# First attention of an eight-sublayer kernel: two score passes in one loop over head pairs, float32r parts in 64-row halves, values for four heads at a time

## Chip, cores and metric

One Trainium2 chip, one of its cores. The metric is the time of one execution on the device, in microseconds (us). The kernel before took 2060.26 us (median of 3 runs, 2055.55 to 2063.94).

## The reference, cut to what matters

The program applies eight sublayers to x (8 batches of 256 rows of 256). The change touches the first one alone:

```python
xn = layernorm(x)                                   # (8, 256, 256)
qh = (xn  @ Wq.T + bq) in 16 heads of 16
kh = (ctx @ Wk.T + bk) in 16 heads of 16
vh = (ctx @ Wv.T + bv) in 16 heads of 16
scores = einsum('bhqd,bhkd->bhqk', qh, kh) / sqrt(16)
scores = where(mask[:, None] == 0, -1e10, scores)
x = x + softmax(scores) @ vh (heads side by side) @ Wo.T + bo
```

Then come a routed feed-forward layer with 8 experts, a causal attention with 16 heads of 64, a second expert layer, a product without softmax, a linear layer, an attention with one head of 256, and a quantised feed-forward layer with a convolution.

## The kernel before

Each sublayer is a stage of its own with a block of engine programs and a barrier behind it. The first attention is `attention0`; a layer norm stands before it and one behind it. It works on one batch of 256 rows at a time. TensorE is written `pe`, VectorE `dve`, ScalarE `act`, GpSimd `pool` and SyncE `sp`.

**Parts.** Queries and keys are projected in float32 (`project`, L313) and split into three bfloat16 parts (high L447, rest L499, middle L452, low L505). DMAs stack copies of the parts on top of each other, six bands of 16 rows per head, so that one product over 96 rows gives a score to nearly float32 accuracy (`to_stack`, L228: 12 DMAs for queries on SP's queue, 12 for keys on GpSimd's).

**Two score passes.** The softmax's maxima are needed before its exponentials. Pass one (`scores`, L338) makes scores with queries on the partitions; a product of an identity with a bfloat16 mask (L340) adds a huge negative number where the mask is zero; DVE reduces each pair of heads (a unit, 8 units in a batch) to its row maxima (L523). The maxima are turned (L347), split into three bfloat16 rows (L457 to L532) and moved by DMA under the stacked queries (`shift_rows`, L263). Pass two (`weigh`, L363 with the mask at L365) makes the scores again, transposed, with the maximum already subtracted by those rows; ACT takes exponentials out of PSUM into `pT` (L467), one unit at a time.

**Values.** For each unit, products of `V` with `pT` (L376) give 32 columns of output per head. Two heads of a unit go to two different column groups of TensorE. One column of V is one, so that it gives the softmax's sum. DVE takes the four banks' worth out in two copies (L541), DMAs turn the sums (L269), DVE inverts them (L515), DMAs put them back as rows (L273), a product with `sel` spreads them (L384), DVE multiplies (L550), and the output projection (L391) is added to x (L557).

**Order.** In a batch TensorE runs: project the next batch, `weigh` for this batch, `scores` for the next, spread the sums, turn the next batch's maxima, output. PSUM banks 0 to 3 are two pairs for a unit each, and both passes alternate between them. Loops over pairs of batches (`Fori`) hold the first six batches; stacked parts, masks and V have two buffers.

Of the kernel before, what the change touches and what calls it, by code (L numbers as in the profile page):

```python
# [21 lines left out]
P = 128  # L22
B, S, D = 8, 256, 256
DK = D // P
# [141 lines left out]
def attention0(nc, top, x, xt, io, consts):  # L166

    G, NG, W = 4, H // 4, 32
    U = H // 2
    PARTS = ((0, 0, 0, 1, 1, 2), (0, 1, 2, 0, 1, 0))
    R = len(PARTS[0]) * D0  # L180
    LAND = 16 * 2 * len(PARTS[0])
    HB = P // D0
    with top.stage() as ctx:
        def sb(name, shape, dt=F32):
# [9 lines left out]
        neg, negT = sb("neg", [P, 2, TB, S], BF16), sb("negT", [P, 2, TB, S], BF16)  # L194
        part = sb("part", [P, 3, 2, DK, S], BF16)
        rest = sb("rest", [P, 2, DK, S])
        qs, ks = sb("qs", [P, 2, H, S], BF16), sb("ks", [P, 2, H, S], BF16)
        V = sb("V", [P, 2, TB, H, W])
        top_s = sb("top_s", [P, TB, H])
        mpart, mrest = sb("mpart", [H, 3, S], BF16), sb("mrest", [H, S])  # L200
        pT = sb("pT", [P, 2, 2, TB, S])
# [4 lines left out]
        O = ps[:, 4:6, :].rearrange("p a (c n) -> p (a c) n", c=2)  # L206

        (weights, ctx_in0, ctx_in1, mask_in, ones_set, q_proj, k_proj, v_proj, hi_done, rest_done, mid_done, lo_done,
         stacked, v_out, neg_ready, s_ready, max_done, mt_ready, mhi_done, mrest_done, mmid_done, mlo_done,
         mrow_landed, st_ready, exp_done, pv_done, o_out, sums_landed, recip_landed, l_ready, recip_done, norm_done,  # L210
         wo_ready, resid_done) = (
             top.semaphore("a0_" + n) for n in (
                 "weights", "ctx_in0", "ctx_in1", "mask_in", "ones_set", "q_proj", "k_proj", "v_proj", "hi_done",
                 "rest_done", "mid_done", "lo_done", "stacked", "v_out", "neg_ready", "s_ready", "max_done",
                 "mt_ready", "mhi_done", "mrest_done", "mmid_done", "mlo_done", "mrow_landed", "st_ready",
                 "exp_done", "pv_done", "o_out", "sums_landed", "recip_landed", "l_ready", "recip_done", "norm_done",
                 "wo_ready", "resid_done"))
        gate, gate_set = sb("gate", [1, 4]), top.semaphore("a0_gate_set")
# [4 lines left out]
        def to_stack(engine, w, n, s):  # L223

            for t, which in enumerate(PARTS[w]):
                if which == n:
                    for k in range(DK):
                        engine.dma_start((qs, ks)[w][t * D0:(t + 1) * D0, s, k * HB:(k + 1) * HB, :],  # L228
                                         part[:, n, w, k, :]).then_inc((stacked, k_stacked)[w], 16)

        def every_batch(engine, body):

            with engine.Fori(0, B // 2 - 1) as pair:
                body(pair * 2, 0, pair, False)
                body(pair * 2 + 1, 1, pair, False)
            body(B - 2, 0, B // 2 - 1, False)
            body(B - 1, 1, B // 2 - 1, True)

        @block.sync
        def _(sp):  # L240
            sp.sem_inc(stacked, 16)
            sp.sem_inc(mrow_landed, 16)

            def load(b, s):
                sp.wait_ge(v_proj, b + 1)
                sp.dma_start(ctxT[:, s, :, :], io["ctxT"][bass.ds(b, 1)].rearrange("b (k p) s -> p (b k) s", p=P)
                             ).then_inc(ctx_in[s], 16)
                sp.wait_ge(neg_ready, b + 1)
                sp.dma_start(mask[:, :, :], io["mask"][bass.ds(b, 1)].rearrange("b (t p) s -> p (b t) s", p=P)
                             ).then_inc(mask_in, 16)  # L250
                sp.dma_start(maskT[:, :, :], io["maskT"][bass.ds(b, 1)].rearrange("b (t p) s -> p (b t) s", p=P)
                             ).then_inc(mask_in, 16)

            def stack(b, s):

                for n, ready in enumerate((hi_done, mid_done, lo_done)):
                    sp.wait_ge(ready, b * 2 + 1)
                    to_stack(sp, 0, n, s)

            def shift_rows(b, s):  # L260
                sp.wait_ge(mlo_done, b + 1)
                for n in range(3):
                    sp.dma_start(qs[R + n:R + n + 1, s, :, :], mpart[:, n, :]).then_inc(mrow_landed, 16)  # L263

            def turn_sums(b):

                sp.wait_ge(o_out, b * 2 + 2)
                for g in range(G):
                    sp.dma_start(sums[g * W:(g + 1) * W, :], oraw[g * W + D0:g * W + D0 + 1, :, :]  # L269
                                 ).then_inc(sums_landed, 16)  # L270
                sp.wait_ge(recip_done, b + 1)
# [4 lines left out]
            def feed(b, s):  # L276

                sp.wait_ge(pv_done, b * U + 2)
                stack(b + 1, 1 - s)
                turn_sums(b)  # L280
                shift_rows(b + 1, 1 - s)

            for dst, name in ((wq, "a0_wq"), (wk, "a0_wk"), (wv, "a0_wv"), (wo, "a0_wo")):
                sp.dma_start(dst[:, :, :], io[name].rearrange("k p n -> p k n")).then_inc(weights, 16)
            sp.dma_start(bqk[:, :, :], io["a0_bqk"]).then_inc(weights, 16)
            for dst, name in ((bv, "a0_bv"), (sel, "a0_sel")):
                sp.dma_start(dst[:, :], io[name]).then_inc(weights, 16)
            load(0, 0)
            load(1, 1)
            stack(0, 0)  # L290
            shift_rows(0, 0)
            with sp.Fori(0, B // 2 - 1) as pair:
                for s in range(2):
                    load(pair * 2 + (2 + s), s)
                    feed(pair * 2 + s, s)
            feed(B - 2, 0)
            turn_sums(B - 1)

        @block.tensor
        def _(pe):  # L300
            pe.sem_inc(v_proj, 2)
            pe.sem_inc(pv_done, 2)
            pe.sem_inc(l_ready, 1)
            pe.sem_inc(wo_ready, 1)
            pe.wait_ge(weights, 16 * 7)

            def project(b, s, half, left=1):
                pe.wait_ge(ctx_in[s], half * 16 + 16)
                pe.wait_ge(norm_done, left)
                for n, (w, src, done) in enumerate(((wq, xt, q_proj), (wk, ctxT, k_proj))):  # L310
                    for c in range(DK):
                        for k in range(DK):
                            mm = pe.matmul(ps[:, 6 + n, c * S:(c + 1) * S], w[:, k, c * P:(c + 1) * P],  # L313
                                           xt[:, k, bass.ds(b * S, S)] if src is xt else ctxT[:, s, k, :],
                                           start=(k == 0), stop=(k == DK - 1))
                    mm.then_inc(done, 1)
                pe.wait_ge(rest_done, b * 2 + 1)
                for t in range(TB):
                    for k in range(DK):
                        mm = pe.matmul(ps[:, 6, t * S:(t + 1) * S], ctxT[:, s, k, t * P:(t + 1) * P], wv[:, k, :],  # L320
# [3 lines left out]
            def scores(b, s, before):  # L324

                pe.wait_ge(stacked, (b + 1) * LAND + 16)
                pe.wait_ge(k_stacked, (b + 1) * LAND)
                pe.wait_ge(neg_ready, b + 2)
                pe.wait_ge(ones_set, 5)
                for u in range(U):  # L330
                    if u >= 2:
                        pe.wait_ge(max_done, b * U + (u - 1))
                    elif before is not None:
                        pe.wait_ge(exp_done, before * U + (U - 1 + u))
                    for j in range(2):
                        h, bank = 2 * u + j, ps[:, 2 * (u % 2) + j, :]
                        for t in range(TB):
                            pe.matmul(bank[:, t * S:(t + 1) * S], qs[0:R, s, h, t * P:(t + 1) * P], ks[0:R, s, h, :],  # L338
                                      start=True, stop=False)
                            mm = pe.matmul(bank[:, t * S:(t + 1) * S], consts["identb"][:, :], neg[:, s, t, :],  # L340
                                           start=False, stop=True)
                    mm.then_inc(s_ready, 1)

            def turn_maxima(b):
                pe.wait_ge(max_done, b * U + U)
                for t in range(TB):
                    mm = pe.transpose(ps[0:H, 4, t * P:(t + 1) * P], top_s[:, t, :], consts["ident"][:, :])  # L347
# [1905 lines left out]
```

## Time and profile before

| | |
|---|---|
| median of 3 runs | 2060.26 us |
| the profiled execution's own time | 2058.89 us |
| its span in the profile | 2057.0 us |
| mean granted TensorE clock | 0.881 |
| PE, PEld busy (share of the span) | 1567.8 us (76%), 1342.9 us (65%) |
| DVE, ACT, POOL busy | 874.1 us (42%), 551.1 us (27%), 337.0 us (16%) |
| first attention, first DMA to last DVE instruction | 28.56 to 368.28 us |

PE is TensorE's matmuls, PEld its weight loads. Busy shares are over the whole span; the first attention is about a sixth of it. PEclk is the granted TensorE clock as a share of 2.4 GHz. A float32 matmul of the program appears as two MATMUL records. The "x8" of a row counts records.

### The profile page before, as it was taken

To read this page: it belongs to the slowest core of one execution; us is meant where nothing else is said; L and a number is where in the kernel's file an instruction comes from. 1 tells how busy PE (TensorE), PEld (TensorE's weight loads), DVE (VectorE), ACT (ScalarE), POOL (GpSimd) and SP (SyncE) were. 2 spreads that over 40 slices of the span, in tenths; PEclk is the share of its full clock that TensorE was granted. 3 is DMA by queue.
4 is the path that set the end of the run, shared out by engine and by line. 5 is a ranking of instruction groups with operands and counts; after the bars stand their busy time and mean duration, and the time that the engine had idled before them with its cause. 6 is when DMAs were issued, how large, how long until landed. Compare 5 with 4: busy or idle time off the path is not lost. (4 is left out here: it accounts for less than half of the span.)

```text
span 2057.0 us, 32700 instructions
## 1 busy us (share of the span) xinstructions
PE 1567.8 (76%) x11346; PEld 1342.9 (65%) x11346; DVE 874.1 (42%) x1913; ACT 551.1 (27%) x1311; POOL 337.0 (16%) x401
## 2 busy tenths in 40 slices
PE   2799997539991699999994099999999256691775
PEld 2465564429991588888884099999999245581664
DVE  5453542402224566666665011111111235548896
ACT  1233232102211455444441011111111011221553
POOL 1112120020002333232321400000000511004122
PEclk8899999569996799999995599999999668795787
DMA  4344241158132200000003454224470210101000
GB/s 123 62 74 67 48 67 14 59 197 275 41 112 77 70 6 7 7 7 2 2 1 113 147 196 148 99 70 147 148 270 18 76 43 20 34 26 41 6 16 21
DMA packets 118240, 152.13 MB, mean 74 GB/s; under 512 B 15360, under 2 KB 101376, under 8 KB 118016
## 3 DMA queue, kind: packets, MB, share of 16 engines
q1 hardware_dynamic: 101536, 123.86, 19.6%
q0 software_dynamic: 7680, 18.89, 4.2%
q10 hardware_dynamic: 8928, 8.13, 1.1%
q8 instruction: 56, 0.92, 0.2%
q14 instruction: 40, 0.33, 0.1%
HBM read 113.16 MB, written 24.64 MB: 67 GB/s over the span
## 5 line engine op out<-in xcount | busy, mean ns | idle before, releaser
L1271 PE MATMUL f_ph<-f_xgT,f_w 128*128 128x128 f32 x3232 | 375.2, 277 | 19.0 <-DMA f_w<-in_f_w 17.8
L1271 PEld LDWEIGHTS f_ph<-f_xgT,f_w 128*128 128x128 f32 x3232 | 373.8, 194 | 24.2 <-issue 21.4
L1281 PE MATMUL f_py<-f_w,f_hT 128*128 128x256 f32 x992 | 224.5, 379 | 0.0
L1281 PEld LDWEIGHTS f_py<-f_w,f_hT 128*128 128x128 f32 x992 | 183.7, 190 | 22.6 <-issue 0.2
L1342 DVE TENSOR_TENSOR f_hT<-f_ph,f_gate_o 128x512 f32<-128x512 f32 x78 | 53.9, 691 | 309.7 <-ACT f_gate_o L1305 309.7
L1376 POOL DMA_INDIRECT c_yt<-sorted_y,dest x48 | 45.6, 949 | 653.2 <-issue 653.2
L799 ACT ACTIVATE a_work<-a_ps,a_bias 128x128 f32<-128x128 f32 (+1 forms) x256 | 104.1, 419 | 145.4 <-DVE a_bias L879 128.2
L937 POOL TENSOR_TENSOR a_work<-a_work,a_recip 128x256 f32<-128x256 f32 (+1 forms) x128 | 103.1, 826 | 233.1 <-DVE a_recip L894 233.1
L145 PE MATMUL n_tp<-ident,n_xn 128*128 128x128 f32 x160 | 32.2, 371 | 135.2 <-DVE n_xn L125 134.5
L1305 ACT ACTIVATE f_gate_o<-f_ph 128x512 f32<-128x512 f32 x78 | 46.6, 597 | 295.2 <-PE f_ph L1271 295.1
L145 PEld LDWEIGHTS n_tp<-ident,n_xn 128*128 128x128 f32 x160 | 24.7, 189 | 143.1 <-DVE n_xn L125 136.1
L1260 PE MATMUL f_px<-ident,f_xg 128*128 128x128 f32 x124 | 24.3, 278 | 90.6 <-DMA f_xg<-sorted_x 90.6
L899 DVE TENSOR_TENSOR a_qk<-a_ps,a_qk 128x512 fp32r<-128x512 f32 x64 | 44.2, 691 | 103.9 <-ACT a_qk L818 103.9
L523 DVE TENSOR_REDUCE a_top_s<-a_ps 128x4 f32<-128x1024 f32 x64 | 75.7, 1214 | 16.7 <-PE a_ps L340 15.9
L467 ACT ACTIVATE a_pT<-a_ps 128x1024 f32<-128x1024 f32 x64 | 64.6, 1023 | 57.6 <-PE a_ps L365 57.6
L338 PE MATMUL a_ps<-a_ks,a_qs 96*128 96x256 bf16 x256 | 62.1, 280 | 22.9 <-DMA a_qs<-a_part 13.5
L1260 PEld LDWEIGHTS f_px<-ident,f_xg 128*128 128x128 f32 x124 | 15.7, 144 | 91.1 <-DMA f_xg<-sorted_x 91.1
L1349 DVE TENSOR_SCALAR f_hT<-f_ph,f_b 128x128 f32<-128x128 f32 x92 | 25.9, 344 | 114.6 <-PE f_ph L1271 114.6
L1173 POOL DMA_INDIRECT sorted_x<-xn,dest x48 | 46.4, 966 | 168.8 <-DVE dest L1149 154.8
L376 PE MATMUL a_ps<-a_pT,a_V 128*32 128x256 f32 x512 | 67.7, 385 | 2.8 <-ACT a_pT L467 1.8
L661 PE MATMUL a_ps<-a_src,a_wq_high 128*128 128x256 f32 x256 | 53.4, 291 | 17.4 <-DVE a_wk_low L843 14.6
L876 DVE TENSOR_REDUCE a_top_s<-a_ps 128x2 f32<-128x256 f32 (+1 forms) x128 | 64.4, 544 | 5.3 <-PE a_ps L724 5.3
(307 smaller groups left out, 3104.8 us busy)
## 6 DMA issues: line engine op xcount, KB each, us to landing
f_w<-in_f_w SPq DMA_DIRECT2D x72, 1024.0 KB, 7.1
f_xg<-sorted_x SPq DMA_DIRECT2D x62, 128.0 KB, 2.1
sorted_y<-f_yg ACTq DMA_DIRECT2D x62, 128.0 KB, 1.7
a_qs<-a_part SPq DMA_DIRECT2D x96, 64.0 KB, 5.2
a_ks<-a_part POOLq DMA_DIRECT2D x96, 64.0 KB, 5.5
sorted_x<-zeros SPq DMA_DIRECT2D x1, 4992.0 KB, 16.4
a_ctxT<-in_ctxT SPq DMA_DIRECT2D x16, 256.0 KB, 2.8
sorted_x<-zeros SPq DMA_DIRECT2D x1, 2944.0 KB, 10.2
```

The source lines that it names most:

```text
L145: mm = pe.transpose(tp[:, b % SLOTS, k, t * P:(t + 1) * P], xn[:, row if router else row % (SLOTS * TB), k * P:(k + 1) * P], ident[:, :])
L338: pe.matmul(bank[:, t * S:(t + 1) * S], qs[0:R, s, h, t * P:(t + 1) * P], ks[0:R, s, h, :], start=True, stop=False)
L376: mm = pe.matmul(O[W * (g0 + j):W * (g0 + j + 1), n, :], V[:, s, t, 4 * n + g0 + j, :], pT[:, m % 2, j, t, :], start=(t == 0), stop=(t == ...
L467: act.activation(pT[:, u % 2, :, :, :].rearrange("p j t n -> p j (t n)"), ps[:, 2 * (u % 2):2 * (u % 2) + 2, :], ACT.Exp, scale=float(D0) ...
L523: dve.tensor_reduce(top_s[:, :, 2 * u:2 * u + 2].rearrange("p t j -> p j t"), ps[:, 2 * (u % 2):2 * (u % 2) + 2, :].rearrange("p j (t k) - ...
L661: mm = pe.matmul(out, left[a][c], right[b][c], start=start and i == 0, stop=stop and i == len(todo) - 1)
L799: act.activation(prob[:, s, i, t * P:(P if t == 0 else TRI)], ps[:, SB + 2 * s + i, t * S:(t * S + P * (t + 1))], ACT.Exp, bias=bias[:, s, ...
L876: dve.tensor_reduce(top_s[:, s, t, :], ps[:, SB + 2 * s:SB + 2 * s + 2, t * S:t * S + P * (t + 1)], AX.X, ALU.max).then_inc(max_done, 1)
L937: pool.tensor_tensor(part, part, recip[:, s, t, :].unsqueeze(2).to_broadcast([P, 2, P * (t + 1)]), ALU.mult).then_inc(shares_done, 1)
L1271: mm = pe.matmul(ph[:, q, n, f * P:(f + 1) * P], w[:, s, k, (q * FQ + f) * P:(q * FQ + f + 1) * P], xgT[:, s, k, :], start=(k == 0), stop= ...
L1281: mm = pe.matmul(py[:, s, 0:D], hT[:, s, f, :], w2[:, s, f, :], start=(f == 0), stop=(f == FT - 1))
L1342: dve.tensor_tensor(hT[:, s, q * FQ:(q + 1) * FQ, :].rearrange("p f n -> p (f n)"), ph[:, q, 1, :], gate_o[:, q, :], ALU.mult).then_inc(h_ ...
```

## The change

- One loop over steps k, written out (no `Fori`), holds both score passes. In step k pass two works on unit k and pass one on unit k + 9 (`AHEAD`), so maxima run one batch and a unit ahead. Each pass has one pair of banks (`SC` and `ST`): pass one of a unit waits for DVE's reduction of the unit before (`max_done`), pass two for ACT's exponential (`exp_done`).
- The mask's products come first (`shut`, four bfloat16 matmuls a pass) and the scores are added on top (`pairs`).
- Queries and keys are split into two float32r parts instead of three bfloat16 parts, in three bands of 16 rows: 48 rows (50 with the maxima, now two rows). The two heads of a unit lie at partitions 0 to 47 and 64 to 111 and their products alternate. 6 + 6 stacking DMAs of 128 KB replace 12 + 12 of 64 KB.
- `weigh` takes four heads at a time, four times a batch, in four column groups.
- The rest of a batch's work (projections of batch i + 2, sums and output of batch i - 1, reciprocals, residual) is dealt out to the eight steps of batch i on every engine. Stacks, masks and V have three buffers.
- At the start DVE no longer fills `ks` with ones; GpSimd fills the whole of it. The weights for values and output load behind the first context and mask.

The lines that are replaced stand in the listing above. What the engines run instead:

```diff
+    HALF, ROWS = P // 2, 3 * D0
+    AHEAD = U + 1
+    PARTS = ((0, 0, 1), (0, 1, 0))
+    ST, SC, OB, MB = 0, 2, 4, 6
...
         def to_stack(engine, w, n, b):
             for t, which in enumerate(PARTS[w]):
                 if which == n:
+                    for j in range(DK):
+                        engine.dma_start((qs, ks)[w][j * HALF + t * D0:j * HALF + (t + 1) * D0, b % 3, :, :].bitcast(F32),
+                                         part[:, n, w, j, :].bitcast(F32)).then_inc((q_stacked, k_stacked)[w], 16)
...   sync
+            for i in range(-2, B + 1):
+                if is_batch(i - 1):
+                    turn_sums(i - 1)
+                if is_batch(i + 2):
+                    stack(i + 2)
+                if is_batch(i - 1):
+                    spread_rows(i - 1)
+                if is_batch(i + 3):
+                    load_mask(i + 3)
+                if is_batch(i + 3) and i + 3 >= 2:
+                    load_ctx(i + 3)
+                if is_batch(i + 1):
+                    shift_rows(i + 1)
...   tensor
+            def shut(first, which, b):
+                for j in range(2):
+                    for t in range(TB):
+                        pe.matmul(ps[:, first + j, t * S:(t + 1) * S], consts["identb"][:, :], which[:, b % 3, t, :],
+                                  start=(t == 0), stop=False, skip_group_check=True)
+            def pairs(first, left, right, rows, b, u):
+                for t in range(TB):
+                    for j in range(2):
+                        r = slice(j * HALF, j * HALF + rows)
+                        mm = pe.matmul(ps[:, first + j, t * S:(t + 1) * S], left[r, b % 3, u, t * P:(t + 1) * P],
+                                       right[r, b % 3, u, :], start=False, stop=True, skip_group_check=True)
+                return mm
+            def scores(k):
+                m = k + AHEAD
+                if is_unit(m):
+                    ...
+                    if m >= 1:
+                        pe.wait_ge(max_done, m)
+                    shut(SC, neg, m // U)
+                if is_unit(k):
+                    if k >= 1:
+                        pe.wait_ge(exp_done, k)
+                    shut(ST, negT, k // U)
+                if is_unit(m):
+                    ...
+                    pairs(SC, qs, ks, ROWS, m // U, m % U).then_inc(s_ready, 1)
+                if is_unit(k):
+                    if k % U == 0:
+                        pe.wait_ge(mrow_landed, (k // U + 1) * 64)
+                    pairs(ST, ks, qs, ROWS + 2, k // U, k % U).then_inc(st_ready, 1)
+            def weigh(b, n):
+                pe.wait_ge(exp_done, b * U + (2 * n + 2))
+                ...
+                for t in range(TB):
+                    for g in range(G):
+                        mm = pe.matmul(O[W * g:W * (g + 1), n, :], V[:, b % 3, t, G * n + g, :],
+                                       pT[:, n % 2, g, t, :], start=(t == 0), stop=(t == TB - 1))
+            def spread_sums(b):
+                pe.wait_ge(recip_landed, (b + 1) * (16 * G))
+                ...
+            for k in steps:                      # range(-2 * U, B * U + 6)
+                i, u = k // U, k % U
+                scores(k)
+                if u == 0 and is_batch(i + 2):
+                    queries(i + 2)
+                if u == 1 and is_batch(i + 2):
+                    keys(i + 2)
+                if u == 3 and is_batch(i - 1):
+                    spread_sums(i - 1)
+                if u in (2, 4, 6) and is_batch(i):
+                    weigh(i, u // 2 - 1)
+                if u in (4, 5) and is_batch(i - 1):
+                    output(i - 1, u - 4)
+                if u == 6 and is_batch(i + 1):
+                    turn_maxima(i + 1)
+                if u == 7 and is_batch(i + 2):
+                    values(i + 2)
+                if u == 7 and is_batch(i):
+                    weigh(i, NG - 1)
...   gpsimd
+            pool.memset(ks[:, :, :, :].bitcast(F32), 1.0).then_inc(set_done, 1)
...   scalar
+                if is_unit(k):
+                    exps(k)
+                if u == 0 and is_batch(i + 2):
+                    high(i + 2, 0, q_proj, q_high)
+                if u == 1 and is_batch(i + 2):
+                    high(i + 2, 1, k_proj, k_high)
+                if u == 6 and is_batch(i + 1):
+                    split_maxima(i + 1)
...   vector
+                if is_unit(k + AHEAD):
+                    maximum(k + AHEAD)
+                if u == 0 and is_batch(i + 2):
+                    low(i + 2, 0, q_high, q_low)
+                if u == 1 and is_batch(i + 2):
+                    low(i + 2, 1, k_high, k_low)
+                if u == 1 and is_batch(i - 1):
+                    reciprocals(i - 1)
+                if u == 2 and is_batch(i + 2):
+                    prepare(i + 2)
+                if u == 3 and is_batch(i - 1):
+                    normalise(i - 1)
+                if u == 4 and is_batch(i):
+                    take_out(i, 0)
+                if u == 5 and is_batch(i - 1):
+                    residual(i - 1)
+                if u == 6 and is_batch(i + 1):
+                    split_maxima(i + 1)
+                if u == 7 and is_batch(i + 2):
+                    add_bias(i + 2)
+                if u == 7 and is_batch(i):
+                    take_out(i, 1)
```

## Rows read from the trace of the kernel before

**Rows 1.** Windows: length, busy PE, PEld, DVE, ACT, POOL (records), clock, DMA share, GB/s.

```profile
28.50:58.50 30.00, 7.65 (x24) 5.92 (x24) 14.03 (x14) 2.82 (x6) 7.11 (x16) 0.67 0.76 156
77.20:334.60 257.40, 241.11 (x1644) 155.01 (x1641) 122.94 (x168) 81.60 (x109) 45.12 (x102) 1.00 0.40 62
302.00:314.00 12.00, 11.78 (x98) 6.88 (x95) 2.41 (x4) 6.53 (x7) 6.07 (x14) 1.00 1.03 121
```

**Rows 2.** Timeline of PE, one batch: start, length (us), line, operands, records.

```profile
264.56 0.27 PE L363 MATMUL a_ps<-a_qs,a_ks 99*128 99x256 bf16 x1
...
296.43 1.89 PE L313 MATMUL a_ps<-xt,a_wq 128*128 128x256 f32 x8
...
302.07 0.27 PE L363 MATMUL a_ps<-a_qs,a_ks 99*128 99x256 bf16 x1
302.19 0.27 PE L365 MATMUL a_ps<-a_negT,identb 128*128 128x256 bf16 x1
...
306.23 1.06 PE L376 MATMUL a_ps<-a_pT,a_V 128*32 128x256 f32 x8
307.22 0.28 PE L363 MATMUL a_ps<-a_qs,a_ks 99*128 99x256 bf16 x1
...
318.33 0.28 PE L338 MATMUL a_ps<-a_ks,a_qs 96*128 96x256 bf16 x1
...
327.72 1.88 PE L384 MATMUL a_ps<-a_rrow,a_sel 128*128 128x512 f32 x4
329.44 0.38 PE L347 MATMUL a_ps<-ident,a_top_s 128*16 128x128 f32 x2
330.39 3.72 PE L391 MATMUL a_ps<-a_wo,a_onorm 128*128 128x256 f32 x16 [0.57 <-DVE a_onorm L550]
334.66 0.28 PE L363 MATMUL a_ps<-a_qs,a_ks 99*128 99x256 bf16 x1 [0.55 <-DMA a_qs<-a_mpart]
```

**Rows 3.** Timeline of PE cut to 308.22 to 308.30.

```profile
308.21 0.41 PE L376 MATMUL a_ps<-a_pT,a_V 128*32 128x256 f32 x2
```

**Rows 4.** Timeline of PE in the third sublayer, causal attention.

```profile
897.01 0.22 PE L717 MATMUL a_ps<-tri,identb 128*128 128x128 bf16 x1
897.16 0.97 PE L724 MATMUL a_ps<-a_qk 64*128 64x256 f32 x12
898.06 0.50 PE L661 MATMUL a_ps<-a_wv_high,a_src 128*128 128x512 f32 x1
```

**Rows 5.** The same, cut to 897.30 to 897.35.

```profile
897.16 0.39 PE L724 MATMUL a_ps<-a_qk 64*128 64x256 f32 x2
```

**Rows 6.** Groups by line, 60 to 520: busy, mean ns, idle before.

```profile
L523 DVE TENSOR_REDUCE a_top_s<-a_ps 128x4 f32<-128x1024 f32 x64 | 75.7, 1214 | 16.7 <-PE a_ps L340 15.9
L467 ACT ACTIVATE a_pT<-a_ps 128x1024 f32<-128x1024 f32 x64 | 64.6, 1023 | 57.6 <-PE a_ps L365 57.6
L499 DVE SCALAR_TENSOR_TENSOR a_rest<-a_ps,a_bqk,a_part 128x256 f32<-128x256 f32 x28 | 12.3, 480 | 13.2 <-ACT a_part L447 13.2
```

**Rows 7.** SP's queue, one batch.

```profile
299.36 7.72 SPq L228 DMA_DIRECT2D a_qs<-a_part  x12
...
323.32 2.45 SPq L273 DMA_DIRECT2D a_rrow<-a_recip  x4
```

**Rows 8.** DMA issues, 296 to 334: KB each, median us to landing.

```profile
a_rrow<-a_recip SPq DMA_DIRECT2D x4, 4.0 KB, 1.7
```

**Rows 9.** Timeline of PE, the stage's start.

```profile
37.42 3.75 PE L313 MATMUL a_ps<-xt,a_wq 128*128 128x256 f32 x8 [9.89 <-DMA a_ctxT<-in_ctxT]
...
58.58 0.37 PE L338 MATMUL a_ps<-a_ks,a_qs 96*128 96x256 bf16 x1 [13.51 <-DMA a_qs<-a_part]
...
77.27 0.27 PE L363 MATMUL a_ps<-a_qs,a_ks 99*128 99x256 bf16 x1
```

**Rows 10.** Timeline of all engines, the stage's end.

```profile
348.75 2.24 PE L376 MATMUL a_ps<-a_pT,a_V 128*32 128x256 f32 x16
...
367.59 0.69 DVE L557 TENSOR_TENSOR x<-a_ps,x 128x512 f32<-128x512 f32 x1 [3.81 <-PE a_ps L391]
```

More of the change, by code:

```diff
@@ L239, in _ @@
+        steps = range(-2 * U, B * U + 6)
         @block.sync
         def _(sp):
[L241 to L252, printed above, removed]
@@ L291, in _ @@
[L291 to L297, printed above, removed]
+            load_ctx(1)
+            for i in range(-2, B + 1):
[11 more added lines that the diff above has]
+                    shift_rows(i + 1)
@@ L299, in _, with project @@
         @block.tensor
         def _(pe):
[L301 to L317, printed above, removed]
+            def project(w, which, src, done):
+                for c in range(DK):
+                    for k in range(DK):
+                        mm = pe.matmul(ps[:, MB + which, c * S:(c + 1) * S], w[:, k, c * P:(c + 1) * P], src[k],
+                                       start=(k == 0), stop=(k == DK - 1))
+                mm.then_inc(done, 1)
@@ new lines, in queries, with keys @@
+            def queries(b):
+                if b == 0:
+                    pe.wait_ge(weights, 16 * 7)
+                if b >= 4:
+                    pe.wait_ge(resid_done, b - 3)
+                project(wq, 0, [xt[:, k, b * S:(b + 1) * S] for k in range(DK)], q_proj)
+            def keys(b):
+                pe.wait_ge(ctx_in[b % 2], 16 * (b // 2 + 1))
+                if b >= 1:
+                    pe.wait_ge(v_out, b)
+                project(wk, 1, [ctxT[:, b % 2, k, :] for k in range(DK)], k_proj)
@@ L385, in spread_sums @@
                               start=True, stop=True).then_inc(l_ready, 1)
-            def output(b):
-                pe.wait_ge(norm_done, b * 2 + 3)
-                for t in range(TB):
-                    for n in range(NG):
-                        mm = pe.matmul(ps[:, 5, t * S:(t + 1) * S], onorm[:, n, t * P:(t + 1) * P], wo[:, n, :],
-                                       start=(n == 0), stop=(n == NG - 1))
-                mm.then_inc(wo_ready, 1)
-            def batch(b, s, half, last):
-                if not last:
-                    project(b + 1, 1 - s, half + s, b * 2 + 1)
-                weigh(b, s)
-                if not last:
-                    scores(b + 1, 1 - s, b)
-                pe.wait_ge(v_out, b + 1 if last else b + 2)
-                pe.wait_ge(lo_done, b * 2 + 2 if last else b * 2 + 4)
-                spread_sums(b)
-                if not last:
-                    turn_maxima(b + 1)
-                output(b)
@@ L408, in _, with output @@
-            project(0, 0, 0)
-            scores(0, 0, None)
-            turn_maxima(0)
-            every_batch(pe, batch)
+            def output(b, t):
+                if t == 0:
+                    pe.wait_ge(norm_done, b * 2 + 2)
+                for n in range(NG):
+                    mm = pe.matmul(ps[:, MB, t * S:(t + 1) * S], onorm[:, n, t * P:(t + 1) * P], wo[:, n, :],
+                                   start=(n == 0), stop=(n == NG - 1))
+                if t == TB - 1:
+                    mm.then_inc(wo_ready, 1)
@@ L427, in batch, with stack @@
-            def batch(b, s, half, last):
-                if not last:
-                    pool.wait_ge(pv_done, b * U + 2)
-                    stack(b + 1, 1 - s)
-            every_batch(pool, batch)
+            def stack(b):
+                if b >= 3:
+                    pool.wait_ge(st_ready, (b - 2) * U)
+                pool.wait_ge(k_high, b + 1)
+                to_stack(pool, 1, 0, b)
+                pool.wait_ge(k_low, b + 1)
+                to_stack(pool, 1, 1, b)
+            pool.memset(ks[:, :, :, :].bitcast(F32), 1.0).then_inc(set_done, 1)
@@ L434, in _ @@
+            pool.wait_ge(set_done, 1)
+            for b in range(B):
+                stack(b)
         @block.scalar
@@ L436, in _, with high @@
             act.wait_ge(weights, 16 * 7)
[L438 to L452 removed]
+            def high(b, n, proj, done):
+                act.wait_ge(proj, b + 1)
+                if b >= 1:
+                    act.wait_ge((q_stacked, k_stacked)[n], b * LAND)
+                for c in range(DK):
+                    a = act.activation(part[:, 0, n, c, :], ps[:, MB + n, c * S:(c + 1) * S], ACT.Identity,
+                                       bias=bqk[:, n, c:c + 1])
+                a.then_inc(done, 1)
@@ L457, in split_maxima @@
-                act.mul(mpart[:, 0, :], ps[0:H, 4, 0:S], -1.0).then_inc(mhi_done, 1)
-                act.wait_ge(mrest_done, b + 1)
-                act.activation(mpart[:, 1, :], mrest[:, :], ACT.Copy).then_inc(mmid_done, 1)
-            def batch(b, s, half, last):
-                if not last:
-                    split(b + 1)
-                for u in range(U):
-                    act.wait_ge(st_ready, b * U + (u + 1))
-                    act.wait_ge(pv_done, b * U + (u + 1))
-                    act.activation(pT[:, u % 2, :, :, :].rearrange("p j t n -> p j (t n)"),
-                                   ps[:, 2 * (u % 2):2 * (u % 2) + 2, :], ACT.Exp,
-                                   scale=float(D0) ** -0.5).then_inc(exp_done, 1)
-                if not last:
-                    split_maxima(b + 1)
@@ L473, in _ @@
-            split(0, first=True)
-            split_maxima(0)
-            every_batch(act, batch)
+                if b >= 1:
+                    act.wait_ge(mrow_landed, b * 64)
+                act.mul(mpart[:, 0, :], ps[0:H, OB, 0:S], -1.0).then_inc(mhi_done, 1)
+            for k in steps:
+                i, u = k // U, k % U
+                if is_unit(k):
[6 more added lines that the diff above has]
+                    split_maxima(i + 1)
@@ L503, in prepare, with low @@
-                for n in range(2):
-                    dve.wait_ge(mid_done, b * 2 + (n + 1))
-                    dve.tensor_tensor(part[:, 2, n, :, :], rest[:, n, :, :], part[:, 1, n, :, :], ALU.subtract
-                                      ).then_inc(lo_done, 1)
-                dve.wait_ge(v_proj, b + 3)
-                dve.wait_ge(ones_set, 5)
-                dve.tensor_tensor(V[:, s, :, :, 0:D0], ps[:, 6, :].rearrange("p (t h w) -> p t h w", t=TB, h=H),
+            def low(b, n, ready, done):
+                dve.wait_ge(ready, b + 1)
+                for c in range(DK):
+                    a = dve.scalar_tensor_tensor(out=part[:, 1, n, c, :], in0=ps[:, MB + n, c * S:(c + 1) * S],
+                                                 scalar=bqk[:, n, c:c + 1], in1=part[:, 0, n, c, :],
+                                                 op0=ALU.add, op1=ALU.subtract)
+                a.then_inc(done, 1)
@@ L517, in maxima, with maximum @@
-            def maxima(b, before):
-                for u in range(U):
-                    if u == 3 and before is not None:
-                        reciprocals(before)
-                    dve.wait_ge(s_ready, b * U + (u + 1))
-                    dve.tensor_reduce(top_s[:, :, 2 * u:2 * u + 2].rearrange("p t j -> p j t"),
-                                      ps[:, 2 * (u % 2):2 * (u % 2) + 2, :].rearrange("p j (t k) -> p j t k", t=TB),
-                                      AX.X, ALU.max).then_inc(max_done, 1)
+            def maximum(m):
+                dve.wait_ge(s_ready, m + 1)
+                if m % U == 0 and m:
+                    dve.wait_ge(mt_ready, m // U)
+                dve.tensor_reduce(top_s[:, :, :, m % U].rearrange("p t j -> p j t"),
+                                  ps[:, SC:SC + 2, :].rearrange("p j (t k) -> p j t k", t=TB),
+                                  AX.X, ALU.max).then_inc(max_done, 1)
@@ L552, in batch, with residual @@
                                       ALU.mult).then_inc(norm_done, 1)
-                if not last:
-                    split_maxima(b + 1)
-                dve.wait_ge(wo_ready, b + 2)
-                xs = x[:, bass.ds(b * TB, TB), :]
-                dve.tensor_tensor(xs, ps[:, 5, :].rearrange("p (t d) -> p t d", t=TB), xs, ALU.add
-                                  ).then_inc(resid_done, 1)
-            prepare(0, 0, 0)
-            maxima(0, None)
-            split_maxima(0)
-            every_batch(dve, batch)
+            def residual(b):
+                dve.wait_ge(wo_ready, b + 1)
+                xs = x[:, b * TB:(b + 1) * TB, :]
+                dve.tensor_tensor(xs, ps[:, MB, :].rearrange("p (t d) -> p t d", t=TB), xs, ALU.add
+                                  ).then_inc(resid_done, 1)
@@ new lines, in _ @@
+            for k in steps:
+                i, u = k // U, k % U
+                if is_unit(k + AHEAD):
[20 more added lines that the diff above has]
+                    take_out(i, 1)
```

279 lines of the change are left out of this document (118 added, 161 removed).

## The prediction

> **What bounds the kernel now.** I read the page's groups first, to find the stage's lines, then the timeline of PE over one batch, then the timelines of the queues, then the windows. In the first attention TensorE is the bound: over 257 us of it PE is busy 241 us at the full granted clock, 2.4 GHz [rows 1]. The reader should see in the batch's landmarks [rows 2] that a batch lasts 302.07 - 264.56 = 37.51 us and how it divides: second score pass with values 318.33 - 302.07 = 16.26; first score pass 327.72 - 318.33 = 9.39; sums spread 1.72; turned maxima and the wait behind them 0.95; output 330.39 to the next batch, 3.55 where the next projection follows; projections 302.07 - 296.43 = 5.64. These add up to 37.51.
> Inside the second pass a unit lasts 1.98 us: eight bfloat16 matmuls at 0.11 each (302.07 to 302.19), with the change to the values 0.99 (307.22 to 308.21), and eight value records 0.99 (306.23 to 307.22) [rows 2, 3]. The first pass needs only 8 x 8 x 0.112 = 7.2 us of matmuls; the rest of 9.39 is waiting for DVE, whose reduction takes 1.21 a unit [rows 6].
>
> **Scores.** Both passes go from 16 bfloat16 matmuls a unit (1.79 us) to 8 for the masks (0.90) and 8 on half the rows. The third sublayer runs just this form: float32r, 64 rows, 256 columns, two halves alternating over two banks. Two such records start together [rows 5], and 12 take 0.90 us from their first to the next line's start, 0.075 each, where a lone one would take at least 0.11 [rows 4]. The price is at the edges: 0.15 us from the last full-row matmul's start to the first half-row start, not 0.112 or less, and some 0.2 behind the last pair. Those 12 are six slots, of which the first is long: I take 0.22, then 0.115 each, then 0.21, which gives 0.22 + 4 x 0.115 + 0.21 = 0.89. A step here has four slots: 7 x 0.112 + 0.15 + 0.22 + 2 x 0.115 + 0.21 = 1.59 us, against 1.79. Saved 0.2 a unit, 1.6 a batch. Bounds: four slots without edges, 0.46, so 1.36 a step; or no overlap of the halves, 8 x 0.216 (the spacing of a float32 record: 1.89 less one length of 0.38, over 7 [rows 2]), so 2.6 a step.
> Such edges are what "TensorEngine Tiling (Array Packing)" of the Trainium skill, section Key Properties, warns of: a change of tiling mode drains the engine. The change adds two a step, some 140 in all. The trace agrees in kind (0.15 and 0.2 us, above) and the sum above already pays it; the page gives no price.
>
> **Values.** Today two records, one of each head of a unit, start at once [rows 3], in four slots of about 0.22 for a unit. With four column groups the same four slots serve two units: 1.08 us with the change of form, four times a batch, 4.3 us against 8 x 0.99 + 8 x 0.1 = 8.7. No row shows four column groups at once. Bounds: all four together, 1.08; no more than two at once, 8 x 0.216 + 0.2 = 1.94. I take the lower, since the two-wide records overlap without loss.
> "TensorE: Matmul & The Clock Gate" of the Trainium skill, Part 3, gives 2.38 times for three column groups. Scaled to four that is an estimate of 3.2 times, 16 x 0.216 / 3.2 = 1.09 and 0.2 of edges instead of 1.08, which would cost 32 x 0.2 = 6.4 us more than I take. No run here shows it yet.
>
> **The rest of TensorE's batch** is unchanged: projections 24 x 0.216 plus edges 5.3, sums 1.72, maxima 0.3, output 3.5, together 10.8. The sum is 12.7 + 4.3 + 10.8 = 27.8 us a batch if it never waits.
>
> **What it now waits for.** There is one pair of banks for each pass, so a step can't begin before DVE has reduced the last unit. From the first mask product: 7 x 0.112 + 0.15 + 0.22 + 0.28 (a length) = 1.43 to the scores' end, 1.23 for the reduction, 0.05 to the next step: 2.75 us at least. Steps last 1.59 plus their other work: 3.3 (u = 0, 1, 3, 5), 4.4 (4, 7), 3.0 (6), 2.7 (2). So alone it hides. ACT's exponential (1.02 [rows 6]) hides too.
> DVE's queue is in order, though. In u = 0 behind the reduction stands `low`, which waits for ACT's `high` (two activations, taken at 0.43 each, a little under DVE's 0.48 for the same shape [rows 6]), which waits for the projection (ends 3.5 after the batch's start). So `low` runs 4.4 to 5.2, the next reduction 5.2 to 6.5, the keys' `low` 7.7 to 8.5 (two of 0.48 [rows 6]), reciprocals to 8.8, the reduction of u = 2 until 10.05, where TensorE wants to begin u = 3 at 9.3: 0.8 us lost.
> Then the sums. Behind `reciprocals` at 8.8 SP issues four DMAs in 2.45 us [rows 7], which land 1.7 us later [rows 8]: 13.0. TensorE is at `spread_sums` at 10.1 + 1.6 = 11.7, so it waits 1.3 us at least. In the kernel before these rows travel with empty queues. Here they stand behind the stacks, on the same queue. Those are still 1.5 MB a batch, and today they hold the DMA engines at a share of 1.03 at 121 GB/s [rows 1], which is 13 us; begun at 4.4 they end at 17. Packets are twice as long now (1 KB rows), and the queries' half goes first, on SP. Bounds: 1.3 and 5.6; I take 2.5, nearer to the uncontended rows, as the queries' half is out by about 12. SP itself is free: 6 issues of 0.64 (12 in 7.72 [rows 7]) follow `q_high`, done at 8.2.
> The maxima's four DMAs leave at 26.8 and land by 31, needed 1.3 us into the next batch at 32.3: no wait, with 1 us to spare.
> A full batch is 27.8 + 0.8 + 2.5 = 31.1 us, for 37.5.
>
> **The ends.** Start: DVE's 6.9 us fill of `ks` goes to GpSimd (cost there unknown, 5 to 9 us, beside the weights' landing, before keys are ready). TensorE begins at 37.4 now and first scores at 58.6, when 24 DMAs have landed [rows 9]. After: weights wait behind context and mask, so TensorE begins at about 39; keys are split by 46.4, the 12 DMAs issued by 49 and landed by 54.5. Then the maxima of batch 0 run in eight steps of 2.3, one pair of banks instead of two (8 units in 12 us now), with the projections and splits of batch 1 among them: 3 to 4 us more. Turned maxima, split and rows: first exponential products at about 80 instead of 77.3 [rows 9], a loss of 2.7; bounds -3 and +8.
> Batch 0 has no sums or output: 31.1 - 5.2 - 2.5 = 23.4. Batches 1 to 5: 5 x 31.1 = 155.5. Batch 6 has no projections: 25. Batch 7 has no first pass and is held by the exponential's chain (2.1 us a step) and by the sums in u = 3: 24. Together 228: the last value product ends at 80 + 228 = 308. The tail (copy, sums out, reciprocals, rows, spread, output, residual) is the same in both: 368.28 - 350.99 = 17.3 [rows 10]. End of the stage 325.3 for 368.3, 43 us less. Nothing else in the program changes.
>
> **The sum.** The profiled execution took 2058.89 us (1.4 under the median of 2060.26): 2059 - 43 = 2016. Small edges that I don't see are likelier losses than gains, so I say 2018.
>
> **Rivals.**
> - A: four column groups work no faster than two. 32 x (1.94 - 1.08) = 27.5, 27 of it felt: 2045. For: no row shows four. Against: two overlap fully [rows 3]. Chance 0.12.
> - B: the reciprocals' rows wait for both stacks, and the wait at u = 3 takes the place of the waits removed: 3.1 us more, six times: 2037. For: DMA share 1.03 while stacks move [rows 1]. Against: longer packets. Chance 0.13.
> - C, slower: halves of 48 and 50 rows don't run side by side, or each pair of halves drains. The place is `pairs`; its price up to 2.6 - 1.59 = 1.0 a step. It decides from 43 / 64 = 0.67 us a step upwards; at the full price 2018 + 64 = 2082. Against it stand the two records that start together [rows 5], though those have 64 rows and twelve in a run, not four and four. Chance 0.06.
> - D: the change doesn't interleave: some wait in DVE's order (a `normalise` or `take_out` that stands before a reduction) lays the 1.23 us reduction bare in each step: 8 x 1.3 - 0.8 = 9.6 a batch, 7 batches: 2085. Chance 0.04.
> The forecast has 0.65.
>
> **Range.** The forecast's own: 2003 (no wait for rows, start no later, 2018 - 12 - 3) to 2033. With A and B inside, 2000 to 2050. A change under 0.5% (10 us) can't be told from none: under 2050 counts as faster. Faster 0.86; same 0.06 (A with other losses, mild C); slower 0.08 (C, D).
>
> **What would show it.** Batches 31 us apart between first queries' projections; `pairs` records starting two by two and steps of 1.6 us of TensorE's own; value groups of 16 records in 1.1 us with four starting together; an idle of PE before the spread of 1 to 3 us put down to the DMA of `rrow`; DVE waiting for ACT's `high` twice a batch; the stage ending near 325. If value groups take 1.9, A; if the wait before the spread is over 5, B; if steps take over 2.3 of TensorE's own, C; if PE waits for `max_done` in most steps, D.

## The result, and the profile after

The kernel after takes 2070.36 us (median of 4 runs, 2066.85 to 2071.68), the kernel before 2059.72 (4 runs) on the same chip: ratio 1.0058, interval 1.0040 to 1.0076. By the medians it is 11 us slower where 42 less were forecast.

| | before | after |
|---|---|---|
| span of the profiled execution | 2057.0 | 2065.0 us |
| granted clock | 0.881 | 0.866 |
| PE busy | 1567.8 | 1533.2 us |
| end of the first attention | 368.28 | 384.72 us |

The stage ends 16.4 us later. The unchanged stages behind it ran 8 us shorter in this execution (from the next layer norm's first instruction to the end 1680.0 for 1688.4), and they differ by as much among the profiled executions of the kernels below (1678.4 to 1685.7). Whether the change has a part in this is not shown; so stages are compared by their own times.

TensorE's timeline in the fourth batch, from the masks' products of u = 1 on (start, length, line, operands, records):

```profile
201.03 0.60 PE L331 MATMUL a_ps<-a_neg,identb 128*128 128x256 bf16 x4
201.46 0.60 PE L331 MATMUL a_ps<-a_negT,identb 128*128 128x256 bf16 x4
201.99 0.50 PE L338 MATMUL a_ps<-a_ks,a_qs 48*128 48x256 f32 x4
202.33 0.40 PE L338 MATMUL a_ps<-a_qs,a_ks 50*128 50x256 f32 x4
202.66 1.99 PE L300 MATMUL a_ps<-a_ctxT,a_wk 128*128 128x256 f32 x8
...
206.12 1.07 PE L386 MATMUL a_ps<-a_pT,a_V 128*32 128x256 f32 x16
207.84 0.61 PE L331 MATMUL a_ps<-a_neg,identb 128*128 128x256 bf16 x4 [0.64 <-DVE a_top_s L521]
208.29 0.60 PE L331 MATMUL a_ps<-a_negT,identb 128*128 128x256 bf16 x4
208.82 0.50 PE L338 MATMUL a_ps<-a_ks,a_qs 48*128 48x256 f32 x4
209.16 0.40 PE L338 MATMUL a_ps<-a_qs,a_ks 50*128 50x256 f32 x4
217.60 3.78 PE L399 MATMUL a_ps<-a_rrow,a_sel 128*128 128x512 f32 x4 [8.04 <-DMA a_rrow<-a_recip]
221.17 1.06 PE L331 MATMUL a_ps<-a_neg,identb 128*128 128x256 bf16 x4
222.02 1.06 PE L331 MATMUL a_ps<-a_negT,identb 128*128 128x256 bf16 x4
```

TensorE's own work is what was forecast. A step of both passes lasts 202.66 - 201.03 = 1.63 us (1.59 forecast), sixteen value records have a length of 1.07 and serve four heads, where eight of [rows 2] served two in 1.06. Cut to a hundredth of a microsecond (here in the second batch), the timeline shows four value records under way together, for the two of [rows 3]:

```profile
143.21 0.42 PE L386 MATMUL a_ps<-a_pT,a_V 128*32 128x256 f32 x4
```

Then TensorE stands for 8 us before the spread of the sums, and comes back at the lower clock: the spread takes 3.57 us (217.60 to 221.17), for 1.72 in [rows 2], and the mask products twice theirs. Windows of this batch (length, busy PE, PEld, DVE, ACT, POOL, clock, DMA share, GB/s) show it; the granted clock of the middle one is 0.50, 1.2 GHz, and TensorE had done nothing for 8 us before it:

```profile
207.00:217.60 10.60, 1.91 (x21) 1.24 (x17) 2.68 (x4) 1.29 (x2) 2.27 (x5) 0.78 1.10 135
217.60:223.00 5.40, 5.40 (x12) 2.38 (x12) 1.38 (x2) 0.00 (x0) 0.00 (x0) 0.50 0.24 75
223.00:240.00 17.00, 16.91 (x150) 12.13 (x150) 8.92 (x10) 5.06 (x6) 0.00 (x0) 0.99 0.01 4
```

The engines that move DMAs are full (1.10) over the window in which TensorE waits. SP's and GpSimd's queues in the same batch:

```profile
202.14 3.83 SPq L223 DMA_DIRECT2D a_qs<-a_part  x6
206.73 2.45 SPq L268 DMA_DIRECT2D a_rrow<-a_recip  x4
209.22 0.59 SPq L239 DMA_DIRECT2D a_mask<-in_mask  x1
...
206.10 3.17 POOL L223 DMA_DIRECT2D a_ks<-a_part  x6 [37.30 <-ACT a_part L456]
```

and the rows' median from issue to landing, 1.7 us in [rows 8]:

```profile
a_rrow<-a_recip SPq DMA_DIRECT2D x4, 4.0 KB, 7.6
```

**Where the forecast's 43 us of the stage went.** It ends at 384.7 for 325.3, 59.4 later. Step 0 begins at 90.8 for 80 (10.8). Batch 0 takes 27.5 for 23.4 (4.1). Batches 1 to 5 begin at 118.3, 157.1, 196.8, 237.6, 276.0 and end at 316.1: 197.8 for 155.5 (42.3). Batches 6 and 7 and the tail: 2.2. Of the 42.3, the wait is 38.8 for the 12.5 I allowed (26.3), and the low clock behind it costs up to 1.8 at the spread and 1.0 in the next step: from the spread's start to the next value group 5.0, 6.1, 6.2, 5.5 and 6.2 us pass in the five batches, for 3.5 in e3 below, 12 in all. Some 4 us, 0.8 a batch, are spread over the rest of the sum.

### The profile page after: what moved, and what is told of

Read it like the earlier page. It is cut to its first block and busy times, and to the rows that moved or that the text cites. A ratio compares the mean times of both kernels' runs of the same rounds, so it can differ in the third digit from the quotient of the medians.

```text
span 2065.0 us, 32124 instructions
## 1 busy us (share of the span) xinstructions
PE 1533.2 (74%) x11346; PEld 1324.2 (64%) x11346; DVE 858.1 (42%) x1887; ACT 537.5 (26%) x1285; POOL 314.3 (15%) x329
## 3 DMA queue, kind: packets, MB, share of 16 engines
q8 instruction: 63, 1.03, 0.2%
## 5 line engine op out<-in xcount | busy, mean ns | idle before, releaser
L694 PE MATMUL a_ps<-a_work,a_V 128*64 128x128 f32 x768 | 56.1, 280 | 11.7 <-issue 5.7
L743 PE MATMUL a_ps<-a_qk 64*128 64x256 f32 x768 | 63.2, 297 | 0.0
```

What stands on the lines that cost most here:

```text
L694: mm = pe.matmul(o_ps[i * W:(i + 1) * W, block, :], V[:, c, h + i, :], pT[:, s, i, (c + block) * P:(c + block + 1) * P], start=(c == 0), s ...
L743: mm = pe.matmul(ps[:, SB + 2 * s + i, t * S:(t + 1) * S], qk[r, s, a, 0, t * P:(t + 1) * P], qk[r, s, b, 1, :], start=False, stop=(n == l ...
```

## Experiments

Theory T: the reciprocals' rows queue behind the stacks' 1.5 MB, and the wait and the clock behind it are all that hides the gain. Rival O: they are only issued too late. e1 to e4 shared their runs of the kernel before, 2058.34 us.

**e1_small_stacks**

```diff
+                        some = S if b < 3 else 16
-                        engine.dma_start((qs, ks)[w][..., b % 3, :, :].bitcast(F32), part[:, n, w, j, :].bitcast(F32))
+                        engine.dma_start((qs, ks)[w][..., b % 3, :, 0:some].bitcast(F32), part[:, n, w, j, 0:some].bitcast(F32))
```

> The kernel after with the stacking DMAs of batches 3 to 7 cut to 16 of 256 columns (same number of DMAs and semaphores; the scores of these batches are then computed from stale stacks). Theory T (traffic): TensorE's wait of 8.1 us before the spread of the sums, in batches 1 to 5, and the slow granted clock behind it are there because the DMAs of the reciprocals' rows queue behind 1.5 MB of stacks. Then the rows land some 2 us after the last issue, the wait falls to 1 to 2 us, the clock stays high, a batch lasts 30 to 32 us for 39.5: 5 x 8 = 40 us less than the kernel after, 2025 to 2035. Rival O (order): the rows are late because SP and DVE reach them late; their landing is not the matter, and the time stays at 2065 to 2072.

This kernel leaves out 240 of 256 columns of the stacks of batches 3 to 7, so its scores there are made from stale ones: it serves to time the traffic alone.

2026.49 us, ratio 0.9847 (0.9821 to 0.9872). With the same number of DMAs and the same order the rows land 1.7 us after their issue, and TensorE's wait before the spread falls from 38.8 to 6.5 us over five batches. T holds, O falls. All waits of PE for these rows, 100 to 310 us (total, times, longest), after, then e1:

```profile
PE a_ps L399 <- DMA a_rrow<-a_recip: 38.8, 5, 8.0
```

```profile
PE a_ps L400 <- DMA a_rrow<-a_recip: 6.5, 5, 2.0
```

The clock behind the short waits varies: the spread takes 3.43 us behind one of 1.09 us (granted clock 0.52), and 1.82 behind one of 1.08:

```profile
163.51 3.59 PE L400 MATMUL a_ps<-a_rrow,a_sel 128*128 128x512 f32 x4 [1.09 <-DMA a_rrow<-a_recip]
196.02 1.98 PE L400 MATMUL a_ps<-a_rrow,a_sel 128*128 128x512 f32 x4 [1.08 <-DMA a_rrow<-a_recip]
```

**e2_loads_later**

```diff
+                if is_batch(i + 3) and is_batch(i - 1):
+                    sp.wait_ge(recip_landed, i * (16 * G))
                 if is_batch(i + 3):
                     load_mask(i + 3)
```

> The kernel after with SP's loads of mask and context held until the reciprocals' rows have landed. They are 0.75 of the 2.3 MB of a batch and are issued right behind the rows. Theory T with engines shared by all queued traffic: the rows no longer share with them and land 2 to 5 us sooner, 5 x 3 = 15 us and some clock: 2045 to 2060. Theory T with rows in line behind the stacks alone: no change, 2065 to 2072. Rival O: no change either.

2067.8 us, ratio 1.0043 (1.0024 to 1.0062): like the kernel after within the noise. The wait is 38.2 us for 38.8. The loads issued behind the rows cost them nothing that shows; what is under way when they are issued is left as the cause, and this run doesn't say which half of it.

**e7_keys_later** (run later, beside 2052.12 us of the kernel before)

```diff
                 pool.wait_ge(k_high, b + 1)
+                if b >= 3:
+                    pool.wait_ge(recip_landed, (b - 2) * (16 * G))
                 to_stack(pool, 1, 0, b)
```

> The kernel after, order of SP and DVE untouched, with GpSimd's stack of keys alone held until the reciprocals' rows have landed. It tells which stack the rows wait for. The prediction took it that the queries' half is out by 12 us into the batch: then the wait before the spread falls from 8.1 to 1 to 3 us and the time to 2025 to 2040, and the keys' half, on the other queue, is to blame for the rest. If the rows' own line behind the queries' stack is the matter, the wait stays over 5 us: 2050 to 2065.

2032.54 us, ratio 0.9908 (0.9873 to 0.9943); the wait falls to 9.8 us over five batches:

```profile
PE a_ps L399 <- DMA a_rrow<-a_recip: 9.8, 5, 2.6
```

Without the keys' half under way, the queries' half in front costs the rows some 1.4 us (they land 3.1 us after issue, median, for 1.7). So the forecast was right that the queries' half is out by then (in the kernel after its last packet ends at 209.3, 12.5 us into the batch), and wrong on the other: the keys' stack, on GpSimd's queue and issued in the same microseconds as the rows, makes 29.0 of the 38.8 us. Its last packet ends at 215.9, as the rows' last one does. No run holds the queries' half back alone.

**e3_rows_first**

```diff
-                if is_batch(i + 2):
-                    stack(i + 2)
                 if is_batch(i - 1):
                     spread_rows(i - 1)
+                if is_batch(i + 2):
+                    stack(i + 2)
...   gpsimd: the wait of e7
...   vector
-                if u == 1 and is_batch(i - 1):
+                if u == 0 and is_batch(i - 1):
                     reciprocals(i - 1)
```

> The kernel after with the reciprocals taken in u = 0 behind the queries' low part, SP issuing the four row DMAs before the queries' stack, and GpSimd holding the keys' stack until the rows have landed. Theory T: rows land within 2.5 us of the last issue, well before u = 3, no wait and no slow clock; stacks still land before u = 7. A batch 30 to 32 us: 2022 to 2035. If the stacks now come too late for u = 7, part of it comes back as a wait there: up to 4 us a batch, 2050. Rival O too expects a gain here, but only of the 3 us by which the issue is earlier: 5 x 3 = 15, 2055.

2021.79 us, ratio 0.9827 (0.9804 to 0.9850). In the batches no wait for the rows is left (one of 8.4 us stays behind the last, as in the kernel before), and the clock stays up: the spread takes 1.83 us again (187.82 to 189.65). Its timeline and SP's queue:

```profile
187.82 1.99 PE L399 MATMUL a_ps<-a_rrow,a_sel 128*128 128x512 f32 x4
189.65 0.60 PE L331 MATMUL a_ps<-a_neg,identb 128*128 128x256 bf16 x4
```

```profile
181.81 2.44 SPq L268 DMA_DIRECT2D a_rrow<-a_recip  x4
184.34 3.84 SPq L223 DMA_DIRECT2D a_qs<-a_part  x6
```

Queries' projections start at 118.75, 147.81, 177.74, 206.81 and 235.89: 29.1 us a batch in three of four, for 37.5 before and 31.1 forecast, of which 2.5 were the wait: 28.6 without it. The later stacks bring no wait at u = 7.

**e4_spread_later**

```diff
-                if u == 3 and is_batch(i - 1):
+                if u == 5 and is_batch(i - 1):
                     spread_sums(i - 1)
-                if u in (4, 5) and is_batch(i - 1):
-                    output(i - 1, u - 4)
+                if u in (6, 7) and is_batch(i - 1):
+                    output(i - 1, u - 6)
...   vector: normalise at u = 5, take_out(i, 0) at u = 6, residual at u = 7
```

> The kernel after with the spread of the sums and the normalising moved from u = 3 to u = 5, the output projection to u = 6 and 7, the first copy of the values to u = 6; the DMAs stay as they are. TensorE reaches u = 5 some 7 us later than u = 3, so under theory T, with rows landing 20 us into the batch, 1 to 2 us of the wait of 8.1 are left: 5 x 8 = 40 less, less 5 us in the tail: 2030 to 2045. Rival O: the same, since it moves the reader and not the rows; it is the run that prices the wait without touching the DMAs. If the price of the wait is not what makes the kernel slow, 2065 or more.

2037.72 us, ratio 0.9908 (0.9889 to 0.9926). The rows still take 7.3 us to land, but the wait is 9.2 us over five batches. Covering the wait instead of removing it gives 33 of the 49 us that e3 gains on the kernel after (by the medians, 1.5 of 2.3% by the ratios). The loop is two steps longer for it, so part of the rest is the tail's.

**e6_two_wide** (on e3, as the two behind it)

```diff
+                for g0 in (0, 2):
                   for t in range(TB):
-                    for g in range(G):
+                    for g in (g0, g0 + 1):
```

> e3_rows_first with each value group's products issued for heads 0 and 1 first, then for heads 2 and 3, so that no more than two column groups are in a row: the worth of four at once alone. If four really run side by side and two do in this order, a group takes 1.9 us for 1.0 and the time rises by 32 x 0.86 = 27.5, of which 20 to 27 are felt: 2042 to 2050. If four in a row gave nothing over two, 2019 to 2024.

2020.2 us, ratio 0.9832 (0.9797 to 0.9867): no change, but the edit did not do what it was to do. Sixteen records in this order still last 1.08 us and start four by four, so it says nothing about the worth of four. It shows that this order of heads inside a group costs nothing.

**e8_values_by_unit** (beside 2055.41 us of the kernel before)

```diff
-            def weigh(b, n):
-                pe.wait_ge(exp_done, b * U + (2 * n + 2))
+            def weigh(b, m):
+                n, g0 = m // 2, 2 * (m % 2)
+                pe.wait_ge(exp_done, b * U + (m + 1))
...
-                    for g in range(G):
+                    for g in (g0, g0 + 1):
...   called for unit u - 1 in u = 1 to 6, for units 6 and 7 in u = 7
```

> e3_rows_first with the values undone to the kernel before's form: a value group of 8 records for each unit, two heads in two column groups, in steps u = 1 to 7, instead of 16 records for four heads every second step. If four column groups are worth what the trace's lengths say (16 records in 0.94 to 1.07 us, 8 records in 0.99), 4 groups more a batch cost 4 x 1.0 us: a batch 33 us for 29.1, 32 us in all less what hides in steps that wait for the reduction: 2040 to 2053. If the steps would otherwise wait and the group of four saves nothing, 2018 to 2025.

2037.78 us, ratio 0.9911 (0.9881 to 0.9941), 17 us over e3 by the ratios and under my range. A batch takes 31.9 us (queries' projections at 151.41, 183.32, 215.22, 247.12) for 29.1, 2.8 more and not 4. The edit did only part of what it was to do: the two groups issued back to back in u = 7 run as sixteen records in 1.08 us, so a batch has seven value groups for e3's four, three more of 0.99 us. Some 0.4 of these 3.0 lie where e3 waits for the reduction (0.43 us before u = 3), and edges add some 0.3. Eight records alone, and the sixteen of u = 7:

```profile
164.17 1.06 PE L387 MATMUL a_ps<-a_pT,a_V 128*32 128x256 f32 x8
165.16 0.61 PE L331 MATMUL a_ps<-a_neg,identb 128*128 128x256 bf16 x4
...
244.46 1.08 PE L387 MATMUL a_ps<-a_pT,a_V 128*32 128x256 f32 x16
```

**e5_start_two_pairs** (beside 2052.12 us of the kernel before, as e6)

```diff
+        def bank(m):
+            return ST if m < AHEAD and m % 2 else SC
...
-                    if m >= 1:
-                        pe.wait_ge(max_done, m)
-                    shut(SC, neg, m // U)
+                    if k < 0:
+                        if m >= 2:
+                            pe.wait_ge(max_done, m - 1)
+                    else:
+                        pe.wait_ge(max_done, m)
+                    shut(bank(m), neg, m // U)
```

> e3_rows_first, and before step 0 the first pass alternates between both bank pairs (the second is free until the first exponential). In the kernel after step 0 begins at 90.8 us where I forecast 80; the eight steps before it take 3.1 us each, the reduction laid bare and the clock at its lower level. If the single pair is what makes them long (theory S), they take 1.3 to 2 us: step 0 some 6 to 9 us earlier, 2012 to 2017. If the landing of batch 1's stack or the projections set them (rival), 2019 to 2023 as e3.

2020.32 us, ratio 0.9839 (0.9810 to 0.9868), as e3: the rival holds. The maxima of batch 0 are done 6 us sooner (turned at 79.96, for 85.70 in e3), and then TensorE waits for the keys' stack of batch 1 instead:

```profile
79.96 0.60 PE L376 MATMUL a_ps<-ident,a_top_s 128*16 128x128 f32 x2 [1.33 <-DVE a_top_s L529]
80.34 1.06 PE L334 MATMUL a_ps<-a_neg,identb 128*128 128x256 bf16 x4
85.44 0.79 PE L341 MATMUL a_ps<-a_ks,a_qs 48*128 48x256 f32 x4 [4.03 <-DMA a_ks<-a_part]
```

**e9_start_loads_later** (on e5, beside e8's runs of the kernel before)

```diff
+                if i == -1:
+                    shift_rows(i + 1)
                 if is_batch(i + 3):
                     load_mask(i + 3)
```

> e5_start_two_pairs with SP's loads of batch 2's mask and context moved behind the maxima's rows of batch 0, out of the way of batch 1's stacks. In e5 TensorE stands from 81.4 to 85.4 us for those stacks. If the loads delay them, step 0 comes 2 to 4 us sooner: 2014 to 2018. If the stacks' own 1.5 MB set the landing, 2018 to 2022.

2018.72 us, ratio 0.9826 (0.9794 to 0.9857). The stack is ready at the same time, 85.49. Its DMAs are issued 1.1 us later here (73.15 for 72.07), so the loads cost it about 1 us of 13.4; the other 12.3 are about what the 1.5 MB of both stacks take at 121 GB/s [rows 1], 13 us. e3, e5, e6 and e9 can't be told apart (2018.7 to 2021.8); all of them beat the kernel before by 1.6 to 1.7%, and by the ratios the kernel after by 2.2 to 2.3%.

## Why the prediction was wrong

- **The scores' sum was right**: 1.63 us a step for 1.59. The halves overlap with 48 and 50 rows as with 64, and the edges cost what [rows 4] showed. Rival C is out.
- **The values' sum was right in length** (16 records in 1.07). Its worth, 4.4 us a batch forecast, was not measured whole: e8 undoes three of the four savings, for 2.8. Rival A is out by the length. The figure for three column groups in "TensorE: Matmul & The Clock Gate" of the Trainium skill, Part 3, scaled to four, is an estimate of 1.09 and, with the edges, 0.2 more. The trace agrees without the 0.2: sixteen records last 1.07 in all, edges included.
- **DVE's order was right**: 0.64 us lost at u = 3 for 0.8. Rival D is out.
- **The step that failed**: "I take 2.5, nearer to the uncontended rows, as the queries' half is out by about 12." The wait is 7.8 us in the mean. The bound that I turned down, all 1.5 MB at 121 GB/s, was the right mechanism, and even it was too low: 5.6 us, with the landing at 17. TensorE's wait ends 20.8 us into the batch (217.60 behind 196.84), since the stacks are not begun at 4.4: the queries' half is issued at 5.3 and the keys' half at 9.3. I counted only the half on the rows' own queue. The keys' half on the other queue is moved by the same engines (e7). "Packets are twice as long now" had no row behind it: the stacks' 1.5 MB again take some 13 us, with the engines at 135 GB/s in the window above, loads included, for 121 in [rows 1].
- **A term left out**: what a wait of 8 us does to the clock. The granted clock is 0.50 for the next 3 to 6 us, which costs 12 us in all. The row that could have warned was in the tail of the kernel before, where the same spread took 3.6 us behind a wait of 8.5; I priced every wait by its length alone.

```profile
359.48 3.57 PE L384 MATMUL a_ps<-a_rrow,a_sel 128*128 128x512 f32 x4 [8.50 <-DMA a_rrow<-a_recip]
```

- **Rival B was the right one**, at a chance of 0.13 and a price of 3.1 us a batch over the forecast; the batches are 8.5 over it, 8 of them wait and clock. With that price it would have stood near 2060, outside the range of 2000 to 2050.
- **The start**: 10.8 us later than forecast. First scores at 60.6 and not 54.5, since the stacks of batch 0 need 13 us here too; then the steps before step 0 take up to 3.1 us at a clock of 0.50 (76.6 to 85.9; 0.67 over 58 to 88), where I reckoned 2.3 at the full one. e5 and e9 show that a faster pass there only runs into the next stack.

With the rows first (e3) the kernel takes 2021.8 us for the 2018 forecast, and part of that nearness is luck. Its stage ends at 334.6 for 325.3: batches 1 to 5 take 146.2 us for 155.5, since they have none of the 12.5 us of wait that the forecast allowed, and this hides a start 11.0 later, 2.7 in batch 0 and 4.9 in batches 6, 7 and the tail. What holds is TensorE's own sum: 29.2 us a batch for 28.6.

## What to carry to other kernels

A small DMA on which an engine waits must be costed behind everything that all queues have under way when it is issued, not behind its own queue: add the bytes and divide by the rate that the windows show for that traffic. When work is interleaved, what used to be separated in time now meets in the DMA engines, so order the issues by who waits: rows of 16 KB first, stacks of 1.5 MB that are needed 15 us later behind them. And price a TensorE wait of several microseconds with the slow stretch behind it: 2.3 us on each of the 7.8 us waits here.

## What the runs showed of the hardware that was not expected

- The stacks' 1.5 MB take about 13 us as 24 DMAs of 64 KB (121 GB/s, share 1.03) and as 12 of 128 KB (135 GB/s with the loads beside them, share 1.10).
- Four column groups overlap without loss (in the kernel after four records start within 0.02 us, every 0.22 us), also when the program's order is heads 0, 1, 0, 1, 2, 3, 2, 3 (e6, 1.08 us for sixteen), and when two groups of eight are issued one behind the other (e8, 1.08).
- DMAs of 4 KB took 7.7 us (median) to land beside the stacks and 1.7 us without most of their bytes, with nothing else changed (e1); 3.1 us with the keys' half held back (e7).
- Stretches of the program that no kernel here touches differ by up to 10 us from one profiled execution to the next (1678.4 to 1688.4).
